# A two-layer deformable convolution on one core: eight tiles of the second stage sampled inside the first, the first plan a chunk sooner, and the first weights split per 128 channels

## The reference

```python
def _dcnv2(x, w_off, b_off, w, b, k, pad):
    om = lax.conv_general_dilated(x, w_off, (1, 1), [(pad, pad), (pad, pad)]) + b_off
    oy, ox, mask = om[:, :P], om[:, P:2 * P], jax.nn.sigmoid(om[:, 2 * P:])   # P = k * k taps
    sy, sx = oy + base_y, ox + base_x
    val = _bilinear(x, sy, sx) * mask          # four corners, zero outside the image
    return jnp.einsum('ncphw,ocp->nohw', val, w) + b
h = _bn_lrelu(_dcnv2(x, w_off1, b_off1, w1, b1, 1, 0), g1, bb1, m1, v1)   # 1x1, 512 -> 256
h = _bn_lrelu(_dcnv2(h, w_off2, b_off2, w2, b2, 3, 1), g2, bb2, m2, v2)   # 3x3, 256 -> 512
return x + h
```

## Time and profile before

| | us |
|---|---|
| median of 3 executions (lowest, highest) | 3087.31 (3086.87, 3090.81) |
| the profiled execution, its own time | 3092.68 |
| its span in the profile | 3090.7 |
| PE busy | 2990.6 (97%) |
| DVE busy | 2740.9 (89%) |
| ACT busy | 2494.6 (81%) |
| POOL busy | 1746.9 (57%) |

### The profile page before, as it was taken

One profiled execution on the slowest core, in us unless ns is written; L12 is line 12 of the kernel. 1 busy time (PEld: TensorE's weight loads), 2 busy tenths in 40 slices (PEclk: granted clock), 3 DMA queues, 4 the chain that ended last, 5 costly groups with the idle time before them and its releaser, 6 DMA issues.

```text
span 3090.7 us, 49986 instructions
## 1 busy us (share of the span) xinstructions
PE 2990.6 (97%) x15660; PEld 2476.2 (80%) x15660; DVE 2740.9 (89%) x4740; ACT 2494.6 (81%) x4658; POOL 1746.9 (57%) x1701
## 2 busy tenths in 40 slices
PE   6998888889999999999999999999999999999999
PEld 6997455558888888888888888888888888888889
DVE  5545999979999999999999999999999999999988
ACT  4665677778888888888888888888888888888886
POOL 0001444456666666666666666666666666666662
PEclk9999899989999999999999999999999999999999
DMA  9998999999999999999999999999999999999995
GB/s 319 318 341 308 375 353 347 347 348 401 382 369 386 382 370 385 378 373 385 371 378 386 368 380 388 366 383 386 365 386 381 366 378 365 366 379 359 371 368 184
DMA packets 431233, 1123.45 MB, mean 363 GB/s; under 512 B 42844, under 2 KB 171356, under 8 KB 431120
## 3 DMA queue, kind: packets, MB, share of 16 engines
q0 software_dynamic: 244672, 891.09, 76.0%
q1 hardware_dynamic: 118608, 163.05, 14.7%
q10 hardware_dynamic: 67840, 68.16, 6.4%
HBM read 1002.15 MB, written 137.04 MB: 369 GB/s over the span
## 4 chain that ended last, share of the span: by engine, by line
PE 88%; DVE 7%; DMA 1%; ACT 1%; issue 1%; ACTq 1%; SPq 0%; DVEq 0%
PE psum_t L1315 66%; PE psum_t L1302 11%; PE psum_t L394 5%; PE psum_t L718 4%; DVE arena L865 2%; PE psum_t L703 1%; DMA arena<-w 1%; DVE arena L898 1%; DVE arena L889 1%; ACTq L299 1%; PE psum_t L736 1%; DVE val_lo L513 1%; DVE arena L1234 1%; DVE arena L881 0%; ACT val_hi L412 0%
## 5 line engine op out<-in xcount | busy, mean ns | idle before, releaser
L1169 POOL DMA_INDIRECT arena<-table,plan_in x1521 | 1578.2, 1038 | 842.7 <-DVE arena L1242 386.6
L1315 PE MATMUL psum_t<-val_hi,w_hi 128*128 128x512 f32 (+2 forms) x3096 | 1231.4, 398 | 0.0
L1183 ACT ACTIVATE psum_t<-arena,plan_in 128x512 f32<-128x512 f32 x1521 | 1043.5, 686 | 206.8 <-DVE arena L1234 206.7
L1315 PE MATMUL psum_t<-val_hi,w_lo 128*128 128x512 f32 (+2 forms) x3096 | 1198.9, 387 | 0.0
L1315 PE MATMUL psum_t<-val_lo,w_hi 128*128 128x512 f32 (+2 forms) x3096 | 1196.6, 387 | 0.0
L1234 DVE SCALAR_TENSOR_TENSOR arena<-arena,plan_in,psum_t 128x512 f32<-128x512 f32 x1521 | 1135.7, 747 | 32.1 <-ACT psum_t L1183 32.1
L1315 PEld LDWEIGHTS psum_t<-val_hi,w_lo 128*128 128x128 f32 x3096 | 582.0, 188 | 119.2
L1315 PEld LDWEIGHTS psum_t<-val_lo,w_hi 128*128 128x128 f32 x3096 | 584.0, 189 | 103.6
L1315 PEld LDWEIGHTS psum_t<-val_hi,w_hi 128*128 128x128 f32 x3096 | 583.5, 188 | 103.0
L1249 DVE TENSOR_TENSOR val_lo<-psum_t,val_hi 128x1024 fp32r<-128x1024 f32 (+2 forms) x387 | 467.0, 1207 | 147.5 <-ACT val_hi L1197 147.4
L1197 ACT ACTIVATE val_hi<-psum_t 128x1024 fp32r<-128x1024 f32 (+2 forms) x387 | 388.0, 1002 | 154.1 <-PE psum_t L1302 153.8
(11 more groups left out here) (90 smaller groups left out, 2406.9 us busy)
## 6 DMA issues: line engine op xcount, KB each, us to landing
arena<-x SPq DMA_DIRECT2D x90, 512.0 KB, 8.5
table<-arena ACTq DMA_DIRECT2D x40, 896.0 KB, 8.3
out<-arena SPq DMA_DIRECT2D x136, 256.0 KB, 5.7
table<-arena ACTq DMA_DIRECT2D x40, 768.0 KB, 6.9
arena<-x SPq DMA_DIRECT2D x70, 384.0 KB, 6.3
arena<-table,plan_in POOLq DMA_INDIRECT x1521, 7.0
table<-table SPq DMA_DIRECT2D x32, 512.0 KB, 11.6
arena<-w POOLq DMA_DIRECT2D x2, 2304.0 KB, 13.7
```

The source lines that it names most:

```text
L1169: nc.gpsimd.indirect_dma_start(landing(r, i)[:, :], None, rows, bass.IndirectOffsetOnAxis(ap=row.bitcast(u32), axis=0))\
L1183: nc.scalar.activation(psum_near[:, unit(r, i) % NEARS, :], landing(r, i)[:, 0:2 * C_MID], ACT.Identity, scale=weight(r, i, 0)).then_inc(n ...
L1315: last = nc.tensor.matmul(psum_acc[:, oc, 0:n], a[:, w, oc * P:(oc + 1) * P], b[:, r % 2, kt, 0:n], start=(w == 0 and a is w2_hi and b is ...
```

## The change

It has four parts.

1. `plan(0)` and the small constants before it are made in chunk 10 in place of 11.
2. Tiles 0 to 7 of the second stage are sampled, and activated, within chunks 11 and 12: from slot 146 (tile 3 of chunk 11) on, every second slot has a `near` on ACT, the next slot its `add_far` and `add_upper` on DVE, the one after `add_lower`, and `activate` once a pair is whole. `near` 8 to 11 and `add_far` 8 to 10 take the place of 0 to 3 and 0 to 2 at the end. DVE's second-stage loop begins at tile 8, those of ACT and PE still at step 0, ACT's without `near` up to step 10. `plan(1)` comes at step 14.
3. The eight tiles lie in two buffers that the third stage uses later, so the `table2` writes of chunk 0 are cut at tiles 4 and 8: 8 DMAs in place of 4. PSUM banks of the first stage's products are six, not seven, with waits changed to fit.
4. The weights are folded and split in four parts of 128 channels, part 0 before the first `lower`, the rest behind it; the bias (three operations) moves behind tile 2. PE awaits each part for itself, the w2 load all four.

```diff
-NEAR_AHEAD = 4
-FAR_AHEAD = 3
-PLAN_AT = 6
+EARLY = 8
+EARLY_AT = (CHUNKS - 2) * CHUNK + 3
+NEAR_AHEAD = EARLY + 4
+FAR_AHEAD = EARLY + 3
+PLAN_AT = EARLY + 6
+NEAR_SLOT = {EARLY_AT + 2 * t: t for t in range(EARLY)}
+NEAR_SLOT.update({TILES - 4 + n: EARLY + n for n in range(4)})
+FAR_SLOT = {at + 1: t for at, t in NEAR_SLOT.items() if at + 1 < TILES}
...
-                pool.wait_ge(w1_scaled, 1)
+                pool.wait_ge(w1_scaled, KT1)
...
-                pe.wait_ge(w1_scaled, 1)
...
-                        pe.wait_ge(y_copied, c * CHUNK + j + 1)
+                        pe.wait_ge(y_copied, c * CHUNK + {3: 6, CHUNK - 1: 6 + 10}.get(j, j + 1))
                         for k in range(KT1):
+                            if j == 0:
+                                pe.wait_ge(w1_scaled, k + 1)
...
-                        if last and j >= CHUNK - NEAR_AHEAD:
-                            near(j - (CHUNK - NEAR_AHEAD))
+                        if early and c * CHUNK + j in NEAR_SLOT:
+                            near(NEAR_SLOT[c * CHUNK + j])
...
-                chunk(CHUNKS - 2, plans=True)
-                chunk(CHUNKS - 1, last=True)
+                chunk(CHUNKS - 3, plans=True)
+                chunk(CHUNKS - 2, early=True)
+                chunk(CHUNKS - 1, early=True, last=True)
...
+                def split_w1(k):
+                    link(nc.vector.tensor_tensor(w1_sb[:, k, 0:C_MID], w1_sb[:, k, 0:C_MID],
+                                                 norm1_sb[:, 0, :], ALU.mult))
+                    link(nc.vector.tensor_copy(w1_hi[:, k, :], w1_sb[:, k, :]))
+                    nc.vector.tensor_tensor(w1_lo[:, k, :], w1_sb[:, k, :], w1_hi[:, k, :].bitcast(f32),
+                                            ALU.subtract).then_inc(w1_scaled, 1)
...
-                    dve.wait_ge(bias_ready, 1)
-                    for t in range(TILES + 1):
+                    for t in range(EARLY, TILES + 1):
...
+                def sample_early(at):
+                    if at in FAR_SLOT:
+                        add_far(FAR_SLOT[at])
+                        if FAR_SLOT[at] < EARLY:
+                            add_upper(FAR_SLOT[at])
+                    if at - 1 in FAR_SLOT and FAR_SLOT[at - 1] < EARLY:
+                        add_lower(FAR_SLOT[at - 1])
+                    if at - 2 in FAR_SLOT and FAR_SLOT[at - 2] < EARLY and FAR_SLOT[at - 2] in PAIR_AT:
+                        activate(PAIR_AT[FAR_SLOT[at - 2]])
```

More of the change, by code:

```diff
@@ L284, in copies_of, with stored_runs @@
             return 2 if c < WHOLE_CHUNKS else 1
+        def stored_runs(c, half):
+            j0, n = HALVES[half]
+            cuts = [j0] + [at for at in (GROUP_TILES, EARLY) if c == 0 and j0 < at < j0 + n] + [j0 + n]
+            return [(a, b - a) for a, b in zip(cuts, cuts[1:])]
         def written_to(b, chunks):
-            return sum(copies_of(c) * 16 for c in range(b, chunks, 2))
+            return sum(copies_of(c) * len(stored_runs(c, 0)) * 16 for c in range(b, chunks, 2))
         def load_plan(sp, s):
@@ L314, in first_stage @@
             w1_scaled = sem("w1_scaled")
+            bias_shifted = sem("bias_shifted")
             om_ready = sem("om_ready")
@@ L331, in y_bank @@
             def y_bank(j):
-                b = j % 7
+                b = (*range(6), *range(6), 3)[j]
                 return psum_t[:, 512 * b:512 * b + N1]
@@ L364, in on_sync @@
                     sp.wait_ge(y_copied, (CHUNKS - 1) * CHUNK + 6 + j0 + n)
-                    table_writes(sp, table1, y_stage, CHUNKS - 1, half, table1_written[half])
+                    table_writes(sp, table1, y_stage[:, j0:j0 + n, :], CHUNKS - 1, j0, n, table1_written[half])
             def on_gpsimd(pool):
@@ L425, in copy_y @@
                             act.wait_ge(y_copied, c * CHUNK + 6 + j0 + n)
-                            table_writes(act, table1, y_stage, c, half, table1_written[half])
+                            table_writes(act, table1, y_stage[:, j0:j0 + n, :], c, j0, n, table1_written[half])
                 def modulation(nth):
@@ L432, in modulation, with chunk @@
                         .then_inc(gate_ready, 1)
-                def chunk(c, first=False, plans=False, last=False):
+                def chunk(c, first=False, plans=False, early=False, last=False):
                     for j in range(CHUNK):
@@ L530, in plan, with chunk @@
                     assert steps[0] == PLAN_STEPS_1, steps
-                def chunk(c, first=False, plans=False, last=False, slabs=()):
+                def chunk(c, first=False, plans=False, early=False, slabs=()):
                     slabs = list(slabs)
                     for j in range(CHUNK):
+                        if first and j == 0:
+                            split_w1(0)
                         lower(c, j)
+                        if first and j == 0:
+                            for k in range(1, KT1):
+                                split_w1(k)
+                        if first and j == 2:
+                            shift(norm1_sb, bias1)
+                            dve.sem_inc(bias_shifted, 1)
                         if first and j == 3:
@@ L542, in chunk @@
                             plan(0)
-                        if last and j >= CHUNK - FAR_AHEAD:
-                            add_far(j - (CHUNK - FAR_AHEAD))
+                        if early:
+                            sample_early(c * CHUNK + j)
                         if slabs and j % 2 == 0 and not (first and j < 6):
@@ L569, in on_vector @@
                 chunk(3, slabs=range(16, 18))
-                with dve.Fori(4, CHUNKS - 2) as c:
+                with dve.Fori(4, CHUNKS - 3) as c:
                     chunk(c)
-                chunk(CHUNKS - 2, plans=True)
-                chunk(CHUNKS - 1, last=True)
+                chunk(CHUNKS - 3, plans=True)
+                chunk(CHUNKS - 2, early=True)
+                chunk(CHUNKS - 1, early=True)
                 return lambda: plan(1)
@@ L595, in h_buf, with h_tiles @@
                 return h_other[:, :, :] if c % 2 else h_stage
+            def h_tiles(c, j, n):
+                if c == 0 and j < EARLY:
+                    buffer = (val_first, val_second)[j // GROUP_TILES]
+                    return buffer.rearrange("p (t c) -> p t c", c=C_MID)[:, j % GROUP_TILES:j % GROUP_TILES + n, :]
+                return h_buf(c)[:, j:j + n, :]
             PAIRS = (CHUNK + 1) // 2
@@ L847, in run @@
                                 act.wait_ge(h_ready, end + j0 + n)
-                                table_writes(act, table2, h_buf(end // CHUNK), end // CHUNK, half,
-                                             table2_written[end // CHUNK % 2][half], copies_of(end // CHUNK))
+                                c = end // CHUNK
+                                for j, rows in stored_runs(c, half):
+                                    table_writes(act, table2, h_tiles(c, j, rows), c, j, rows,
+                                                 table2_written[c % 2][half], copies_of(c))
                         if 0 <= t - TILES - 1 < BEGUN:
@@ L957, in run @@
                     modulate(CHUNKS - 1)
-                return add_far, run
+                def sample_early(at):
[7 more added lines that the diff above has]
+                        activate(PAIR_AT[FAR_SLOT[at - 2]])
+                return sample_early, run
             return on_sync, on_gpsimd, on_tensor, on_scalar, on_vector
@@ L1365, in _ @@
             begin_units, go_on = third_vector(dve)
-            add_far, second = second_vector(dve, begin_units)
-            late_plan = first_vector(dve, add_far)
+            sample_early, second = second_vector(dve, begin_units)
+            late_plan = first_vector(dve, sample_early)
             second(late_plan)
```

42 lines of the change are left out of this document (19 added, 23 removed).

## The result

| | median, us (lowest to highest) | profiled execution | span |
|---|---|---|---|
| changed | 3100.99 (3098.02 to 3102.80) | 3099.38 | 3097.3 |
| before, eight executions | 3089.80 (3086.87 to 3092.66) | 3092.68 | 3090.7 |

The ratio is 1.0036, with the 95% interval [1.0027, 1.0046]: slower by some 11 us. The forecast was 2.6 us less, and its range ended at 3093.5. The profiled execution of the kernel before is slower than each of its eight timed ones, so what the two profiles show against each other is in part the scatter of that one execution.

A forecast was written before the change was run, and what follows sets the result against it. DVE was taken to bound the second stage, PE the third, with PE and DMA nearly full in the first. -14.0 + 5.5 + 0.5 + 5.4 = -2.6 us on 3087.3 gave 3084.7 us, range 3074.5 to 3093.5.

The forecast's parts named there:

- that stage has a fixed length and its end moves with its start: Third stage: PE, busy 20.00 of 20 us, fixes its length, so only its start can move its end.
- Starved writes: Rival, chunks 11 and 12: both awaited table1 writes take 21.2 us to land beside gathers; +12.6 us, 3099.9, chance 0.13.
- First weights: Start of first stage: PE's head start of some 3 us ends in the wait for w2; 0, range 0 to -1.
- The PSUM banks ... also cost 0: First stage: six banks cost 0, as ACT's in-order copies have met their waits by then.
- DVE, ACT and DMA in chunks 10 to 12: End of first stage: early tiles' work just fits with small slips, +0.5 us; writes wait longer beside gathers, +5.4 us.
- upper bound: DMA term, chunks 11 and 12: both awaited writes take the longest landing, 21.2 us, giving +20.6 us.
- Eight tiles: DVE's second stage: eight tiles taken out at 3.49 us per two; -14.0 us.
- the refill: Start of second stage: DVE waits ahead of tile 12 for PE and ACT; +5.5 us, bounds 0 and about 10.
- the four more DMA issues stand beside this wait, so they cost 0: Start of second stage: ACT's four added DMA issues overlap DVE's wait ahead of tile 12; 0.
- no refill wait: Rival, start of second stage: ACT and PE pass their eight steps sooner than counted; -8.1 us, 3079.2, chance 0.11.
- low clock: Rival, start of second stage: PE's matmuls run slower after a long wait; +1.9 us, 3089.2, chance 0.07.
- The stall of ACT's queue in the second stage: Third pair of writes, which held DVE for 4.63 us, stalls again as before; 0, bounds -4.6 and +4.6.

The follow-up runs named there:

- aligned_again: The changed kernel with 48 spare semaphore increments at ACT's start, moving its third-stage loop off the stops; 3091.48 us, ratio 1.0003.
- spread_quiet: The changed kernel with 48 spare semaphore increments on ACT, one per tile in the second stage; 3090.88 us, ratio 1.0004.
- before_pad_quiet: The kernel before with 53 spare semaphore increments on ACT, putting its third-stage loop where the changed kernel has it; 3100.97 us, ratio 1.0036.
- before_all_sp: The kernel before with SP issuing every second-stage table write instead of ACT, and spare increments keeping its third-stage loop in place; 3090.03 us, ratio 1.0002.
- paced: aligned_again with each of POOL's first eight gathers held until ACT has copied the tile six places ahead of its sampling place; 3099.63 us, ratio 1.0033.
- plan_only: The changed kernel with plan and gathers a chunk sooner but no added early tiles, plus spare increments for the loop's place; 3095.92 us, ratio 1.0022.
- after_pad: The changed kernel with 48 spare semaphore increments at ACT's start, run on a slower chip; 3272.78 us, ratio 1.0016 to the kernel before.

## Why the prediction was wrong

**The step that failed** is its first: "that stage has a fixed length and its end moves with its start", said of the third stage from PE's 20.00 of 20 us. True of PE, but it priced the third stage at 0 without asking whether an engine's instructions come as before. The change puts 53 instructions on ACT ahead of an unchanged loop; that cost 10.5 to 11.4 us in place of 0, four times the forecast's whole gain. No rival had it. Starved writes, at 3099.9, came out nearest in time, but the third stage brought the time there, not the writes.

With the stops away (aligned_again, spread_quiet), the ratio is 1.0003 [0.9994, 1.0012] and 1.0004 [0.9995, 1.0013]: no difference from the kernel before can be told, where -2.6 us, a ratio of 0.9992, was forecast. So the front missed its small gain too, and the terms below name where. Term by term, profiled executions against each other:

- **First weights, 0 (0 to -1)**: +1.1 by chunk 9, outside its range, though 0.7 of it come in chunks 1 to 8, where no weights of the first stage are split. "The PSUM banks ... also cost 0" is in doubt: some 0.07 us a chunk are lost where no other part of the change stands. That the head start dies in the wait for w2 was right.
- **DVE, ACT and DMA in chunks 10 to 12, +0.5 and +5.4**: +6.9 in the changed kernel. With the weights, DVE's second stage starts 8.3 us later (309.69 against 301.37), 5.9 forecast; in aligned_again and spread_quiet the last `x_lo` is 11.0 and 9.4 us later than before. The waits were said to be 6.7 and 2.1 us for the two halves; they are 3.8 in all, and 6.4 us of ACT's time go at an *issue*, where the prediction had none. The starved write (19.17 us) is of the size of its upper bound, the second (11.51) is the landing forecast, 11.2. And the plan a chunk sooner brings its burst with or without early tiles: together they are 5.3 of the 6.9. (The upper bound has a slip: 21.2 less 9.1 is 12.1, which gives 20.8 and not 20.6.)
- **Eight tiles, -14.0, and the refill, +5.5**: the wait ahead of tile 12 is 8.21. The step "the four more DMA issues stand beside this wait, so they cost 0" was wrong: with them on SP it is 5.60, the forecast to 0.1 us. PE's transposes and convolution were priced rightly: they end some 8.8 us after DVE's second stage starts (318.5 less 309.7), 8.6 forecast. So "no refill wait" and "low clock" are out.
- **The stall of ACT's queue in the second stage, 0**: it didn't come again at chunk 1, which gave the changed kernel's profile up to 4.6 us. But it is no fixed property of the kernel before either. before_pad_quiet, the same work, has 3.3 us of it, and DVE's second stage takes 334.4 us there (301.2 to 635.6), 338.5 in the profile of before. I worked the sum from one execution whose second stage was 4 us longer than another one's.

By the start of its first `add_upper` and that of its last activation, DVE's second stage runs from 309.7 to 636.0 in the changed kernel and from 301.4 to 639.9 before: 12.2 us shorter. -14.0 + 8.2 is -5.8, the stall -4.6, and -1.8 is left, which no row names. Against before_pad_quiet in place of before the front gains nothing: 665.3 and 665.7. The kernel before starts its third stage at 670.1, 665.7 and 670.5 (before, before_pad_quiet, before_all_sp), a spread as large as the 4.8 us of gain that the first pair of profiles showed.

What stays open: how much of the 9 to 11 us the early gathers take each (paced shows that the bytes have to go somewhere, not a price for one), what the six banks cost, and whether the 3.4 us by which aligned_again starts its third stage later than the changed kernel are more than scatter.

## What to carry to other kernels

A loop that nobody touched can slow down because code ahead of it grew. When an unchanged stage takes longer, look for an engine waiting on "issue" once a round and at the packets of the instruction queue, and move the loop with spare instructions before judging the edit; a difference of 0.36% was made, and unmade, by these alone. When two traces are compared term by term, get a second execution of the kernel before: a term of 4 us here was scatter. And where DMA engines are at a share of 0.99, work moved ahead brings its bytes with it: count what else must land in that stretch, and on whose queue an issue will block.

## What the hardware did that I had not expected

- **A loop of 299 instructions made ACT stop for some 3.5 us a round** (18 stops, 63.3 us) at one place in the stream and not at all at two others, 53 below and 48 above. 90 more instruction packets moved, 0.73 MB.
- **An engine can be held at a DMA issue while its earlier writes are under way**: 6.43 and 4.63 us for ACT at two writes, 6.61 for SP at three, 3.99 for ACT in plan_only, each with writes of its own queue issued 2 to 9 us before and with gathers beside them. From 160 to 235 us of the kernel before, with no gathers about, a pair takes 1.0 us though another went out 9 to 11 us before. How much a queue takes before it holds its engine, no run here tells.
- **The same kernel takes 178 us longer on some chips**: the kernel before took 3089.2 to 3089.9 us in four sets of runs and 3267.5 and 3269.5 in two others; each set whose chip is on record had its own, so the chip isn't told apart from the hour. The front is as long there (667.2 in after_pad), so the 178 us are all in the third stage, where ACT waits for what the profile calls "remote", 209.6 us in 52 times in after_pad. The mean granted clock is a little lower too, 0.979 there and 0.992 in aligned_again, the same kernel. What it is, no run here tells.
